# A routing stage takes over the experts' bias, the copy of x, the spare rows and the first weight load

## The chip, the cores and the metric

The program runs on one NeuronCore of a Trainium2 chip, as one launch. The metric is the device time of that core in microseconds (us), a median over executions. A profile is one execution as the hardware recorded it. The engines are TensorE (PE; its weight loads are PEld), VectorE (DVE), ScalarE (ACT), GpSimd (POOL) and SyncE (SP), which here only issues transfers. They run apart from each other and meet at semaphores.

## The reference

1250 tokens with 768 numbers each go through four residual blocks: a graph attention net, a mixture of experts, a graph convolution net and an attention block with a feed-forward net. The change lies in the second one:

```python
def _L0_ffn_ref(x, router_w, w1, b1, w2, b2):
    E, C, F, K = (8, 768, 384, 2)
    logits = flat @ router_w.T
    probs = jax.nn.softmax(logits.astype(jnp.float32), axis=-1)
    top_w, top_i = jax.lax.top_k(probs, K)
    top_w = (top_w / top_w.sum(-1, keepdims=True)).astype(x.dtype)
    out = jnp.zeros_like(flat)
    for e in range(E):
        w_e = jnp.sum(top_w * (top_i == e), axis=-1)[:, None]
        h = jax.nn.gelu(flat @ w1[e] + b1[e], approximate=False)
        out = out + w_e * (h @ w2[e] + b2[e])

x = x + _L0_ffn_ref(_layernorm(x, axis=-1)[None], L0_ffn_router_w, ...)[0]
```

Each token goes to two of eight experts. The term with `b2` needs no expert's product: for all tokens it is the matrix of weights (1250 x 8) times `b2` (8 x 768).

## The kernel before

The program is a row of stages. A stage (`Phase`) has its own tiles and semaphores, hands each engine a list of instructions, and ends at a barrier of all engines (`ph.end`): no engine starts the next stage before all have finished this one. Inside an engine's list the order is as written; there is no scheduler.

The tokens lie as 10 tiles of 125 rows (`NT`, `TP`). x, the residual, is kept in SBUF. `layernorm_turned` normalizes it, writes the rows to `token_scratch` in DRAM and keeps them turned for the router. Then come the two stages of the change.

`route` (lines 1147 to 1350) computes the logits on PE, the softmax and the two highest experts on DVE, and gives every choice a slot. The slots are cut into parts of 128 rows; two parts (`PER_LOAD`) share one load of an expert's weights, so that there are at most 17 loads and 34 parts. Which expert a load needs is in `load_expert` (L1319). PE turns the weights, and ACT copies them to `weights_T` (L1262) after POOL has cleared that tile (L1206). The last work of the stage is a loop of 20 steps, one for each tile of tokens and choice. In each, DVE builds a one-hot of the row in its part (`row_hot`, L1339) and three one-hots of the part, times the token, times the gate and plain (`part_hot`, L1340 to L1342), and PE adds their product to bank 6 (L1247). There are two buffers: step n of DVE waits until PE has done step n-2 (`placed`). Four small DVE operations (L1346 to L1349) turn the sum into `slot_token`, the list by which rows are gathered and scattered.

`experts` (from L1353) starts with work that isn't an expert's. POOL clears `b2` and `zeros`; SP loads `b2` and stores the zeros as spare rows of `token_scratch` and `sum_scratch`; SP reads `load_expert` and issues the first weights (`w1` L1403, `b1` L1406, `w2` L1409). PE makes 20 products of 384 columns of `weights_T` and `b2` (L1498) in two banks by turns; DVE adds each to x (L1607, semaphore `b2_added`); SP stores each finished tile of x to `sum_scratch` (L82, L83 in `move_rows`). POOL gathers the rows of the first parts (L1431) after the spare rows have landed. PE turns the rows of parts 0 and 1 (L1455), waits for the last of the 20 additions, and starts the first product of part 0 (L103, called by `up`). ACT and DVE split weights into a high and a low part first (L1519 and L1577 for `w1`; L1533 and L1587 for the rows). From there each part runs up, gelu, down, and POOL adds its rows to `sum_scratch` by an indirect DMA (L1444), one after another.

A PE product of two float32 operands is recorded as two LDWEIGHTS and two MATMUL; float32r operands give one of each, and a product of split operands (`product`, L103) has three of those.

Of the kernel before, what the change touches and what calls it, by code (L numbers as in the profile page):

```python
# [7 lines left out]
ALU = mybir.AluOpType  # L8
ACT = mybir.ActivationFunctionType
# [8 lines left out]
N = 1250  # L18
# [1128 lines left out]
def route(nc, g, i):  # L1147
# [4 lines left out]
    ps, ident, xT, weights, weights_T = g["ps"], g["ident"], g["xT"], g["weights"], g["weights_T"]  # L1152
    rw = ph.sb("router_w", [128, KD, EXPERTS])
    logit_T = ph.sb("logit_T", [EXPERTS, N])
    logits_out, cleared = ph.sem("logits_out"), ph.sem("cleared")
# [21 lines left out]
    gate = ph.sb("gate", [TP, 2, NT])  # L1177
# [9 lines left out]
    part_hot = ph.sb("part_hot", [TP, 2, 3, PARTS])  # L1187
    ended = ph.sb("ended", [TP, LOADS, EXPERTS])
# [9 lines left out]
    with ph.block() as block:  # L1198

        @block.sync  # L1200
        def _(sp):
            sp.dma_start(rw[:], i["router_w"]).then_inc(rw_in, 16)

        @block.gpsimd
        def _(pool):
            pool.memset(weights_T[:], 0.0).then_inc(cleared, 1)  # L1206
# [17 lines left out]
        def _(pe):  # L1224
# [19 lines left out]
            pe.matmul(ps[0:TP, 5, 0:NT * EXPERTS], all_ones[:], marks, start=True, stop=True).then_inc(counted, 1)  # L1244
            for n in range(2 * NT):
                pe.wait_ge(hot_ready, n + 1)
                last = pe.matmul(ps[0:PART, 6, 0:3 * PARTS], row_hot[:, n % 2, :], part_hot[:, n % 2].rearrange("p k s -> p (k s)"),  # L1247
                                 start=n == 0, stop=n == 2 * NT - 1)
                last.then_inc(placed, 1)

        @block.scalar
        def _(a):
# [6 lines left out]
            a.wait_ge(cleared, 1)  # L1259
            for b in range(3):  # L1260
                n = 4 if b < 2 else 2
                last = a.activation(weights_T[0:EXPERTS, b * 4 * TP:(b * 4 + n) * TP], ps[0:EXPERTS, 1 + b, 0:n * TP], ACT.Copy)  # L1262
            last.then_inc(turned_out, 1)

        @block.vector
        def _(v):
# [52 lines left out]
            step(v.tensor_copy(load_expert[:], one_load[0:1, :]))  # L1319
            step(v.tensor_tensor(place[:], ps[0:TP, 4, 0:NT * EXPERTS].rearrange("p (t e) -> p t e", e=EXPERTS), start[:, 0:NT, :], ALU.add))  # L1320
# [8 lines left out]
            step(v.tensor_reduce(gate[:], picked[:], AX.X, ALU.add))  # L1329
# [4 lines left out]
            for n in range(2 * NT):  # L1334
# [18 lines left out]
def experts(nc, g, i, x, token_scratch, sum_scratch, ahead):  # L1353
# [4 lines left out]
    ps, ident, weights_T = g["ps"], g["ident"], g["weights_T"]  # L1358
# [7 lines left out]
    b2 = ph.sb("b2", [128, D])  # L1366
    zeros = ph.sb("zeros", [128, D])
# [6 lines left out]
    cleared, b2_in, w1_in, w2_in, b1_in, ahead_in, x_stored, spare_stored = (  # L1374
        ph.sem("cleared"), ph.sem("b2_in"), ph.sem("w1_in"), ph.sem("w2_in"), [ph.sem("b1_in0"), ph.sem("b1_in1")],
        ph.sem("ahead_in"), ph.sem("x_stored"), ph.sem("spare_stored"))
    w1_high, w2_high, w1_split, w2_split = ph.sem("w1_high"), ph.sem("w2_high"), ph.sem("w1_split"), ph.sem("w2_split")
    b2_done, b2_added = ph.sem("b2_done"), ph.sem("b2_added")
# [11 lines left out]
    with ph.block() as block:  # L1390

        @block.sync
        def _(sp):
            sp.wait_ge(cleared, 2)
            sp.dma_start(b2[0:EXPERTS, :], i["moe_b2"]).then_inc(b2_in, 16)
            sp.dma_start(token_scratch[N:N + PART, :], zeros[:]).then_inc(spare_stored, 16)
            sp.dma_start(sum_scratch[N:N + PART, :], zeros[:]).then_inc(spare_stored, 16)

            def load(n):
# [3 lines left out]
                sp.dma_start(w1, i["moe_w1"][bass.ds(e, 1)].rearrange("a (k p) f -> p (a k) f", p=128)).then_inc(w1_in, 16)  # L1403
# [5 lines left out]
                sp.dma_start(w2, i["moe_w2"][bass.ds(e, 1)].rearrange("a (k p) f -> p (a k) f", p=128)).then_inc(w2_in, 16)  # L1409

            load(0)
            for t in range(NT):
                sp.wait_ge(b2_added, 2 * t + 2)
                move_rows(sp, sum_scratch[t * TP:(t + 1) * TP, :], x[:, t, :], x_stored)
            for n in range(1, LOADS):
                load(n)
# [6 lines left out]
        def _(pool):  # L1423
            pool.memset(b2[:], 0.0).then_inc(cleared, 1)
            pool.memset(zeros[:], 0.0).then_inc(cleared, 1)
            pool.wait_ge(spare_stored, 32)
# [9 lines left out]
            for n in range(PARTS):  # L1436
# [3 lines left out]
                if n == 0:  # L1440
                    pool.wait_ge(x_stored, 32 * NT)
# [7 lines left out]
        def _(pe):  # L1449
# [41 lines left out]
            pe.wait_ge(cleared, 1)  # L1491
            pe.wait_ge(b2_in, 16)
            for t in range(NT):
                for j in range(2):
                    n = 2 * t + j
                    if n >= 2:
                        pe.wait_ge(b2_added, n - 1)
# [75 lines left out]
        def _(v):  # L1573
# [29 lines left out]
            for t in range(NT):  # L1603
                for j in range(2):
# [1164 lines left out]
```

## Time and profile before

| | us |
|---|---|
| median of 3 runs | 3139.02 (3132.99 to 3140.41) |
| the profiled execution, its own time | 3143.17 |
| its span in the trace | 3141.4 |
| PE busy in the span | 2598.8 (83%) |
| DVE busy | 1970.2 (63%) |
| ACT busy | 1393.8 (44%) |
| route, from its first POOL operation to its last on DVE | 1405.0 to 1464.2 |
| experts, from its first POOL operation | from 1466.4 |

Times in the trace count from the start of the span. The page of the profile sums each engine over the whole program; the chain of waits at its end covers only the last few per cent, so the two stages have to be read from the timeline and from the busy times of short windows. A stage ends at a barrier, so an engine that finishes early in it gains nothing by itself.

### The profile page before, as it was taken

How to read it: one execution, taken by the hardware profiler on the slowest of the kernel's cores; microseconds unless marked ns; L12 is line 12 of the kernel's file. 1: busy time of each engine (PE TensorE's matmuls, PEld its weight loads, DVE VectorE, ACT ScalarE, POOL GpSimd, SP SyncE). 2: the span in 40 equal slices, each digit the busy share in tenths (PEclk: the TensorE clock that was granted, in tenths of full speed). 3: DMA queues.
4: the chain of work that ended last, by engine and by line, in shares of the span. 5: the costliest groups of instructions: out<-in, count | busy, mean ns of one | idle time of the engine just before them, and what ended most of it. 6: DMA issues, size and time to landing. Idle time of an engine off the chain costs nothing. (4 is left out here: it accounts for less than half of the span.)

```text
span 3141.4 us, 40088 instructions
## 1 busy us (share of the span) xinstructions
PE 2598.8 (83%) x14620; PEld 2306.3 (73%) x14621; DVE 1970.2 (63%) x2887; ACT 1393.8 (44%) x2433; POOL 262.5 (8%) x190
## 2 busy tenths in 40 slices
PE   5774879887986978975999589789897998999876
PEld 5663779787986977963889557467665776999766
DVE  7776278787877843346555342542895556989654
ACT  0353267676775831110666310031896103777330
POOL 0000030040040000000232120000000000111000
PEclk9996989998998988986999779889998997999988
DMA  0023101201111262222899750124661212443304
GB/s 33 16 49 93 42 23 40 64 31 62 41 43 51 63 166 50 49 60 106 249 256 249 176 109 0 49 96 154 140 129 27 94 54 57 106 88 87 93 1 103
DMA packets 107249, 267.12 MB, mean 85 GB/s; under 512 B 11062, under 2 KB 49448, under 8 KB 106090
## 3 DMA queue, kind: packets, MB, share of 16 engines
q1 hardware_dynamic: 99474, 238.26, 27.8%
q0 software_dynamic: 7616, 26.74, 3.9%
q8 instruction: 99, 1.62, 0.2%
q14 instruction: 60, 0.49, 0.1%
HBM read 194.41 MB, written 66.73 MB: 83 GB/s over the span
## 5 line engine op out<-in xcount | busy, mean ns | idle before, releaser
L910 PE MATMUL ps<-h,e_gat_aggregate 125*125 125x193 f32 x2400 | 405.0, 332 | 51.9 <-DVE e_gat_aggregate L892 51.9
L910 PEld LDWEIGHTS ps<-h,e_gat_aggregate 125*125 125x125 f32 x2400 | 398.7, 191 | 58.2 <-DVE e_gat_aggregate L892 58.2
L890 DVE TENSOR_TENSOR e_gat_aggregate<-e_gat_aggregate 125x1250 f32<-125x1250 f32 x120 | 174.7, 1456 | 77.5 <-ACT e_gat_aggregate L861 74.3
L103 PE MATMUL ps<-gat_w_pair_gat_scores,x_turned 128*125 128x384 f32 x1080 | 195.7, 344 | 32.0 <-DVE gat_w_pair_gat_scores L757 31.9
L103 PEld LDWEIGHTS ps<-gat_w_pair_gat_scores,x_turned 128*125 128x125 f32 x1080 | 194.2, 190 | 33.3 <-DVE gat_w_pair_gat_scores L757 33.1
L103 PE MATMUL ps<-w_pair_dense_rows_from,col_dense_rows_from 128*125 128x384 f32 x1080 | 210.5, 352 | 8.3 <-DVE w_pair_dense_rows_from L1088 4.5
L103 PEld LDWEIGHTS ps<-w_pair_dense_rows_from,col_dense_rows_from 128*125 128x125 f32 x1080 | 196.3, 194 | 9.8 <-DVE col_dense_rows_from L1082 7.7
L858 ACT ACTIVATE e_gat_aggregate<-row_gat_aggregate,from_src 125x1250 f32<-125x1250 f32 x120 | 161.7, 1347 | 87.2 <-PE ps L910 62.6
L2448 DVE TENSOR_TENSOR ln_home<-p_attend,p_high_attend 125x1254 fp32r<-125x1254 f32 x120 | 179.9, 1512 | 27.1 <-ACT p_high_attend L2434 24.3
L2426 ACT ACTIVATE p_attend<-ps 125x1254 f32<-125x1254 f32 (+2 forms) x168 | 148.6, 915 | 79.9 <-PE ps L2389 78.1
L1941 DVE TENSOR_SCALAR_CACHE_REDUCE res_attention_statistics<-ps 125x1250 f32<-125x1250 f32 x120 | 173.3, 1459 | 12.2 <-PE ps L1918 6.2
L892 DVE SCALAR_TENSOR_TENSOR e_gat_aggregate<-e_gat_aggregate,count 125x1250 f32<-125x1250 f32 x120 | 175.3, 1461 | 4.2
L103 PE MATMUL ps<-V_home,ln_home 128*125 128x512 f32 x720 | 170.0, 398 | 2.7 <-PEq L54 2.7
L1965 ACT ACTIVATE p_attention_statistics<-res_attention_statistics,eak_attention_statistics 125x1250 bf16<-125x1250 f32 x120 | 160.7, 1339 | 14.8 <-DVE res_attention_statistics L1941 4.3
L508 PE MATMUL ps<-ident,_normed_layernorm_turned 125*128 125x125 f32 x300 | 69.5, 410 | 115.4 <-DVE _normed_layernorm_turned L493 115.3
L766 DVE SCALAR_TENSOR_TENSOR peak_gat_scores<-ps,from_src,peak_gat_scores 125x1250 f32<-125x1250 f32 x108 | 156.6, 1512 | 12.4 <-ACTq L730 12.3
L103 PEld LDWEIGHTS ps<-V_home,ln_home 128*125 128x125 f32 x720 | 135.1, 188 | 36.9 <-issue 2.8
L861 ACT ACTIVATE e_gat_aggregate<-row_gat_aggregate,from_src 125x1250 f32<-125x1250 f32 x120 | 160.1, 1334 | 1.3 <-DMA row_gat_aggregate<-r_scratch 1.3
L103 PE MATMUL ps<-ln_home,V_home 128*128 128x512 f32 (+3 forms) x702 | 142.5, 367 | 14.7 <-DVE V_home L613 14.7
L508 PEld LDWEIGHTS ps<-ident,_normed_layernorm_turned 125*128 125x128 f32 x300 | 55.8, 217 | 129.0 <-DVE _normed_layernorm_turned L493 129.0
L103 PEld LDWEIGHTS ps<-ln_home,V_home 128*128 128x128 f32 (+1 forms) x702 | 118.4, 195 | 38.9 <-DVE V_home L613 15.2
L351 PE MATMUL ps<-dst_hot_build_adjacency,src_hot_build_adjacency 125*125 125x128 bf16 x1600 | 122.8, 230 | 25.9 <-DVE dst_hot_build_adjacency L283 25.9
(388 smaller groups left out, 5119.3 us busy)
## 6 DMA issues: line engine op xcount, KB each, us to landing
stock<-in_moe_w SPq DMA_DIRECT2D x34, 1152.0 KB, 6.9
row_gat_aggregate<-r_scratch SPq DMA_DIRECT2D x24, 625.0 KB, 6.1
V_home<-q_scratch SPq DMA_DIRECT2D x44, 312.5 KB, 6.3
ln_home<-q_scratch SPq DMA_DIRECT2D x36, 312.5 KB
ln_home<-k_scratch SPq DMA_DIRECT2D x36, 312.5 KB
rows_dense_rows_from<-node_scratch SPq DMA_DIRECT2D x8, 1080.0 KB
q_scratch<-V_home SPq DMA_DIRECT2D x6, 1250.0 KB, 4.6
k_scratch<-V_home SPq DMA_DIRECT2D x6, 1250.0 KB, 4.6
```

The lines of the kernel that those rows point to most:

```text
L103: last = pe.matmul(out, left(x), right(y), start=start and n == 0, stop=stop and n == 2)
L508: last = pe.transpose(ps[:, 2 * (t % 4) + k // 4, k % 4 * TP:(k % 4 + 1) * TP], normed[:, t % 3, k * 128:(k + 1) * 128], ident[0:TP, 0:TP])
L766: last = v.scalar_tensor_tensor(peak[:, head, :], far[t % 2], from_src[:, head, t:t + 1], peak[:, head, :], ALU.subtract, ALU.min)
L858: a.activation(e[:, n % 3, 0, :], row[0:TP, head % 2, 0, :], ACT.Exp, bias=from_src[:, head, t:t + 1])
L861: a.activation(e[:, n % 3, 1, :], row[0:TP, head % 2, 1, :], ACT.Exp, bias=from_src02[:, head, t:t + 1]).then_inc(exp_ready, 1)
L890: v.tensor_tensor(e[:, n % 3, 0, :], e[:, n % 3, 0, :], e[:, n % 3, 1, :], ALU.max).then_inc(p_step, 1)
L892: v.scalar_tensor_tensor(e[:, n % 3, 0, :], e[:, n % 3, 0, :], 1.0, count[:, t, 0:N], ALU.min, ALU.mult).then_inc(p_ready, 1)
L910: last = pe.matmul(ps[0:TP, bank(head, d // 2), d % 2 * (C + 1):(d % 2 + 1) * (C + 1)], e[:, n % 3, 0, d * TP:(d + 1) * TP], h[:, t, head, :],
L1941: v.tensor_scalar(minus[:, n % 3, :], flat(n), 1.0, None, ALU.mult, ALU.min, accum_out=peak[:, head, t:t + 1]).then_inc(peaked, 1)
L1965: a.activation(p[:], minus[:, n % 3, :], ACT.Exp, scale=-1.0, bias=peak[:, head, t:t + 1], accum_out=total[:, head, t:t + 1]).then_inc(sum ...
L2426: last = a.activation(spread(p[:, n % AHEAD, :])[:, at:end, :], ps[0:TP, bank:bank + end - at, 0:PIECE], ACT.Exp, scale=-1.0)
L2448: v.tensor_tensor(p_low[:, n % AHEAD, :], p[:, n % AHEAD, :], p_high[:, n % AHEAD, :].bitcast(F32), ALU.subtract).then_inc(split, 1)
```

## The change

The 20 products of weights and `b2` go to `route`. They are no longer added to x by DVE: PE adds x itself, by a product of the identity with x into the same bank (L1272 of the new kernel), and ACT copies the sum back to x (L1300). Eight of the 20 stand before the loop of 20 steps, twelve inside it, each ahead of a step's product. They rotate over four banks. SP loads `b2` (now 8 rows) at the stage's start, stores the spare rows, waits for `load_expert` and issues the first `w1` and `w2`, and then stores x tile by tile; it waits for all stores at the stage's end. In the step of the loop the three one-hots of the part become one `scalar_tensor_tensor` with the factors token, gate and 1, which a MEMSET, a copy and the former reduction of the gates put side by side. `experts` loses its whole preamble and starts with the gathers; only `b1` of the first load is still issued there.

```diff
+            sp.dma_start(b2[:], i["moe_b2"]).then_inc(b2_in, 16)
+            sp.wait_ge(zeroed, 1)
+            sp.dma_start(token_scratch[N:N + PART, :], zeros[:]).then_inc(stored, 16)
+            sp.dma_start(sum_scratch[N:N + PART, :], zeros[:]).then_inc(stored, 16)
+            sp.wait_ge(load_known, 1)
+            e = sp.value_load(load_expert[0:1, 0:1], min_val=0, max_val=EXPERTS - 1)
+            sp.dma_start(stock(g, 0, KD, FF), i["moe_w1"][bass.ds(e, 1)]...).then_inc(g["w1_in"], 16)
+            sp.dma_start(stock(g, KD * FF, FF // 128, D), i["moe_w2"][bass.ds(e, 1)]...).then_inc(g["w2_in"], 16)
+            for t in range(NT):
+                sp.wait_ge(x_out, 2 * t + 2)
+                move_rows(sp, sum_scratch[t * TP:(t + 1) * TP, :], x[:, t, :], stored)
+            sp.wait_ge(stored, 32 + 32 * NT)
...
-            pool.memset(weights_T[:], 0.0).then_inc(cleared, 1)
+            pool.memset(zeros[:], 0.0).then_inc(zeroed, 1)
...
+            def with_bias(n):
+                t, j = n // 2, n % 2
+                if n >= 4:
+                    pe.wait_ge(x_out, n - 3)
+                columns = slice(j * 384, (j + 1) * 384)
+                out = ps[0:TP, X_BANKS[n % 4], 0:384]
+                pe.matmul(out, weights_T[:, t * TP:(t + 1) * TP], b2[:, columns], start=True, stop=False)
+                pe.matmul(out, ident[0:TP, 0:TP], x[:, t, columns], start=False, stop=True).then_inc(x_summed, 1)
+
+            pe.wait_ge(b2_in, 16)
+            pe.wait_ge(turned_out, 1)
+            for n in range(8):
+                with_bias(n)
             for n in range(2 * NT):
+                if n + 8 < 2 * NT:
+                    with_bias(n + 8)
                 pe.wait_ge(hot_ready, n + 1)
...
+            for n in range(2 * NT):
+                a.wait_ge(x_summed, n + 1)
+                a.activation(x[:, n // 2, n % 2 * 384:(n % 2 + 1) * 384], ps[0:TP, X_BANKS[n % 4], 0:384], ACT.Copy).then_inc(x_out, 1)
...
-                v.tensor_scalar(part_hot[:, n % 2, 0], part_iota[:], here, token[:, t:t + 1], ALU.is_equal, ALU.mult)
-                v.tensor_scalar(part_hot[:, n % 2, 1], part_iota[:], here, gate[:, c, t:t + 1], ALU.is_equal, ALU.mult)
-                step(v.tensor_scalar(part_hot[:, n % 2, 2], part_iota[:], here, None, ALU.is_equal))
+                step(v.scalar_tensor_tensor(part_hot[:, n % 2], part_iota[:].unsqueeze(1).broadcast_to([TP, 3, PARTS]), here,
+                                            factor[:, c, t, :].unsqueeze(2).broadcast_to([TP, 3, PARTS]), ALU.is_equal, ALU.mult))
...
-            pe.wait_ge(cleared, 1)
-            pe.wait_ge(b2_in, 16)
-            for t in range(NT):
-                for j in range(2):
...
-                    pe.matmul(ps[0:TP, 6 + j, 0:384], weights_T[:, t * TP:(t + 1) * TP], b2[:, j * 384:(j + 1) * 384],
-                              start=True, stop=True).then_inc(b2_done, 1)
             turn(0)
             turn(1)
-            pe.wait_ge(b2_added, 2 * NT)
...
-            for t in range(NT):
-                for j in range(2):
-                    v.wait_ge(b2_done, 2 * t + j + 1)
-                    here = x[:, t, j * 384:(j + 1) * 384]
-                    v.tensor_tensor(here, ps[0:TP, 6 + j, 0:384], here, ALU.add).then_inc(b2_added, 1)
```

PE's list from the counting of the choices to the first product of an expert, before (x20 stands for the 20 steps, which nothing separates):

```order
238 L1243 MATMUL ps<-either_route,tokens_before_route 125x80
239 L1244 MATMUL ps<-either_route,all_ones_route 125x80
240 L1247 MATMUL ps<-part_hot_route,row_hot_route 128x102 x20
241 L1198 UNCONDITIONAL_BRANCH
242 L1448 UNCONDITIONAL_BRANCH
243 L1498 MATMUL ps<-b_experts,expert_weights_T 125x384 x20
244 L1455 MATMUL ps<-ident,rows_experts 128x128 x12
245 L103 MATMUL ps<-w_pair_experts,rows_turned_experts 128x384 x18
```

And after, where the eight pairs ahead of the loop end and its steps begin:

```order
254 L1271 MATMUL ps<-b_route,weights_turned_route 125x384
255 L1272 MATMUL ps<-x,ident 125x384
256 L1271 MATMUL ps<-b_route,weights_turned_route 125x384
257 L1272 MATMUL ps<-x,ident 125x384
258 L1282 MATMUL ps<-part_hot_route,row_hot_route 128x102
259 L1271 MATMUL ps<-b_route,weights_turned_route 125x384
260 L1272 MATMUL ps<-x,ident 125x384
261 L1282 MATMUL ps<-part_hot_route,row_hot_route 128x102
```

```order
288 L1282 MATMUL ps<-part_hot_route,row_hot_route 128x102
289 L1271 MATMUL ps<-b_route,weights_turned_route 125x384
290 L1272 MATMUL ps<-x,ident 125x384
291 L1282 MATMUL ps<-part_hot_route,row_hot_route 128x102 x9
292 L1204 UNCONDITIONAL_BRANCH
293 L1470 UNCONDITIONAL_BRANCH
294 L1477 MATMUL ps<-ident,rows_experts 128x128 x12
295 L103 MATMUL ps<-w_pair_experts,rows_turned_experts 128x384 x18
```

Steps 0 to 11 now have a pair of 384-column products ahead of their own; the last eight have none; and the turning of rows follows the stage's start directly.

DVE's list at the first step of the loop, before:

```order
605 L1339 TENSOR_SCALAR row_hot_route<-row_iota_route,row_of_route 125x128
606 L1340 TENSOR_SCALAR part_hot_route<-part_iota_route,part_of_route,token_route 125x34
607 L1341 TENSOR_SCALAR part_hot_route<-part_iota_route,part_of_route,gate_route 125x34
608 L1342 TENSOR_SCALAR part_hot_route<-part_iota_route,part_of_route 125x34
609 L1339 TENSOR_SCALAR row_hot_route<-row_iota_route,row_of_route 125x128
```

and after:

```order
607 L1379 TENSOR_SCALAR row_hot_route<-row_iota_route,row_of_route 125x128
608 L1380 SCALAR_TENSOR_TENSOR part_hot_route<-part_iota_route,part_of_route,factor_route 125x102
609 L1379 TENSOR_SCALAR row_hot_route<-row_iota_route,row_of_route 125x128
```

A step has two operations in place of four; the new one covers 102 columns where each of the three old ones covered 34.

## Rows read from the trace of the kernel before

**Rows 1.** Busy time in windows; the column after POOL's is the granted clock.
```profile
1444.20:1463.20 19.00, 14.14 (x38) 9.51 (x38) 15.32 (x72) 0.00 (x0) 0.00 (x0) 0.50 0.00 0
...
1474.40:1486.70 12.30, 12.27 (x33) 4.83 (x33) 8.76 (x16) 2.59 (x6) 1.91 (x2) 1.00 0.98 380
...
1506.00:1545.00 39.00, 35.96 (x222) 35.09 (x221) 23.10 (x40) 25.61 (x51) 12.92 (x10) 1.00 0.91 254
```

**Rows 2.** Timeline (start, length, engine, line), before the loop of steps.
```profile
1433.53 1.30 ACT L1262 ACTIVATE expert_weights_T<-ps 8x500 f32<-8x500 f32 x3 [10.22 <-PE ps L1238]
...
1433.63 0.62 PE L1244 MATMUL ps<-either_route,all_ones_route 125*125 125x80 f32 x2
```

**Rows 3.** Timeline, one step of the loop on DVE and PE.
```profile
1453.64 0.29 DVE L1339 TENSOR_SCALAR row_hot_route<-row_iota_route,row_of_route 125x128 f32<-125x128 f32 x1 [0.15 <-DVE part_hot_route L1342]
...
1454.26 0.24 DVE L1342 TENSOR_SCALAR part_hot_route<-part_iota_route,part_of_route 125x34 f32<-125x34 f32 x1
1454.61 0.50 PEld L1247 LDWEIGHTS ps<-part_hot_route,row_hot_route 125*128 125x128 f32 x2 [0.50 <-DVEq L1343]
...
1454.65 0.29 DVE L1339 TENSOR_SCALAR row_hot_route<-row_iota_route,row_of_route 125x128 f32<-125x128 f32 x1 [0.15 <-DVE part_hot_route L1342]
```

**Rows 4.** Timeline, the end of route and the start of experts.
```profile
1462.62 0.75 PE L1247 MATMUL ps<-part_hot_route,row_hot_route 125*128 125x102 f32 x2 [0.25 <-DVEq L1343]
...
1464.03 0.17 DVE L1349 CAST slot_token<-filled_route 128x34 int32<-128x34 f32 x1
1466.44 0.74 POOL L1424 MEMSET b_experts<- 128x768 f32 x1 [58.33 <-POOLq L54]
...
1476.56 2.59 ACT L1519 ACTIVATE w_pair_experts<-stock 128x384 fp32r<-128x384 f32 x6 [41.73 <-DMA stock<-in_moe_w]
```

**Rows 5.** Timeline, DVE's first two additions of the bias, and PE's first ten matmuls.
```profile
1469.73 5.61 PE L1498 MATMUL ps<-b_experts,expert_weights_T 128*125 128x384 f32 x10 [6.36 <-DMA b_experts<-in_moe_b]
...
1471.38 0.56 DVE L1607 TENSOR_TENSOR x<-ps,x 125x384 f32<-125x384 f32 x1 [7.18 <-PE ps L1498]
...
1472.66 0.56 DVE L1607 TENSOR_TENSOR x<-ps,x 125x384 f32<-125x384 f32 x1 [0.72 <-PE ps L1498]
```

**Rows 6.** Timeline, from the turned rows to the first product of part 0.
```profile
1486.75 0.82 PE L1455 MATMUL ps<-ident,rows_experts 128*128 128x128 f32 x6
...
1487.42 2.89 DVE L1577 TENSOR_TENSOR w_pair_experts<-stock,w_pair_experts 128x384 fp32r<-128x384 f32 x6
...
1487.60 0.87 ACT L1533 ACTIVATE rows_turned_experts<-ps 128x512 fp32r<-128x512 f32 x2 [8.45 <-PE ps L1455]
...
1490.23 1.02 DVE L1587 TENSOR_TENSOR rows_turned_experts<-ps,rows_turned_experts 128x512 fp32r<-128x512 f32 x2
...
1491.39 1.51 PE L1455 MATMUL ps<-ident,rows_experts 128*128 128x128 f32 x6 [3.83 <-DVE rows_turned_experts L1587]
...
1492.56 5.60 PE L103 MATMUL ps<-w_pair_experts,rows_turned_experts 128*128 128x384 f32 x18
```

**Rows 7.** Groups of instructions by shape, whole span: count, busy us, mean ns of one.
```profile
L1743 PE MATMUL ps<-gcn_w,urned_graph_convolutions 128*125 128x384 f32 x80 | 26.9, 491 | 1.8 <-ACT urned_graph_convolutions L1757 1.3 <-DVE x L1797 0.4
...
L283 DVE SCALAR_TENSOR_TENSOR dst_hot_build_adjacency<-ion_iota_build_adjacency,_columns_build_adjacency,e_values_build_adjacency 125x128 bf16 x160 | 54.9, 343 | 0.0
...
L741 ACT ACTIVATE h<-ps 125x384 f32<-125x384 f32 x60 | 29.0, 484 | 29.2 <-PE ps L103 29.2
```

**Rows 8.** Granted clock in short windows, columns as in rows 1.
```profile
1473.25:1473.50 0.25, 0.25 (x2) 0.23 (x1) 0.00 (x0) 0.00 (x0) 0.20 (x1) 0.50 0.82 301
1473.50:1473.75 0.25, 0.25 (x2) 0.19 (x2) 0.00 (x0) 0.00 (x0) 0.25 (x1) 0.94 1.04 393
...
1497.00:1498.00 1.00, 1.00 (x6) 0.84 (x4) 0.47 (x1) 0.31 (x1) 0.00 (x0) 0.79 0.45 167
```

**Rows 9.** The 34 gathers of rows (L1431), us from issue to landing.
```profile
DMA to landing us min/median/max: 4.9/5.7/8.8
```

**Rows 10.** Issue of a plain transfer: KB, us to landing.
```profile
token_scratch<-zeros_experts SPq DMA_DIRECT2D x1, 384.0 KB, 2.3
```

More of the change, by code:

```diff
@@ L1144, with route @@
 PARTS = LOADS * PER_LOAD
-def route(nc, g, i):
+def route(nc, g, i, x, token_scratch, sum_scratch):
     ph = Phase(nc, g, "route")
-    ps, ident, xT, weights, weights_T = g["ps"], g["ident"], g["xT"], g["weights"], g["weights_T"]
+    ps, ident, xT, weights = g["ps"], g["ident"], g["xT"], g["weights"]
+    weights_T = ph.sb("weights_turned", [EXPERTS, N])
+    b2 = ph.sb("b2", [EXPERTS, D])
+    zeros = ph.sb("zeros", [128, D])
+    b2_in, zeroed, load_known, x_summed, x_out, stored = (
+        ph.sem("b2_in"), ph.sem("zeroed"), ph.sem("load_known"), ph.sem("x_summed"), ph.sem("x_out"), ph.sem("stored"))
+    X_BANKS = (7, 1, 2, 3)
     rw = ph.sb("router_w", [128, KD, EXPERTS])
     logit_T = ph.sb("logit_T", [EXPERTS, N])
-    logits_out, cleared = ph.sem("logits_out"), ph.sem("cleared")
+    logits_out = ph.sem("logits_out")
     lower = ph.sb("lower_index", [TP, EXPERTS, EXPERTS])
@@ L1258, in _ @@
             a.wait_ge(turned, 1)
[L1259 removed]
             for b in range(3):
                 n = 4 if b < 2 else 2
[L1262 removed]
+                last = a.activation(weights_T[:, b * 4 * TP:(b * 4 + n) * TP], ps[0:EXPERTS, 1 + b, 0:n * TP], ACT.Copy)
             last.then_inc(turned_out, 1)
+            for n in range(2 * NT):
+                a.wait_ge(x_summed, n + 1)
+                a.activation(x[:, n // 2, n % 2 * 384:(n % 2 + 1) * 384], ps[0:TP, X_BANKS[n % 4], 0:384], ACT.Copy).then_inc(x_out, 1)
         @block.vector
@@ L1328, in _ @@
             step(last)
-            step(v.tensor_reduce(gate[:], picked[:], AX.X, ALU.add))
+            v.memset(factor[:, :, :, 2], 1.0)
+            v.tensor_copy(factor[:, :, :, 0], token[:].unsqueeze(1).broadcast_to([TP, 2, NT]))
+            step(v.tensor_reduce(factor[:, :, :, 1], picked[:], AX.X, ALU.add))
             step(v.tensor_copy(slot_i[:, 0], slot[:]))
@@ L1350, in route, with experts @@
     ph.end()
-def experts(nc, g, i, x, token_scratch, sum_scratch, ahead):
+def experts(nc, g, i, token_scratch, sum_scratch, ahead):
     ph = Phase(nc, g, "experts")
-    ps, ident, weights_T = g["ps"], g["ident"], g["weights_T"]
+    ps, ident = g["ps"], g["ident"]
     slot_token, slot_gate, load_expert = g["slot_token"], g["slot_gate"], g["load_expert"]
@@ L1408, in load @@
                     sp.wait_ge(w2_split, KF * n)
-                sp.dma_start(w2, i["moe_w2"][bass.ds(e, 1)].rearrange("a (k p) f -> p (a k) f", p=128)).then_inc(w2_in, 16)
-            load(0)
-            for t in range(NT):
-                sp.wait_ge(b2_added, 2 * t + 2)
-                move_rows(sp, sum_scratch[t * TP:(t + 1) * TP, :], x[:, t, :], x_stored)
-            for n in range(1, LOADS):
+                    sp.dma_start(w2, i["moe_w2"][bass.ds(e, 1)].rearrange("a (k p) f -> p (a k) f", p=128)).then_inc(w2_in, 16)
+            for n in range(LOADS):
                 load(n)
@@ L2647, in build @@
             g["weights"] = tile(moe, "expert_weights", [TP, NT, EXPERTS])
-            g["weights_T"] = tile(moe, "expert_weights_T", [128, N])
+            g["w1_in"] = moe.enter_context(nc.semaphore("first_layer_in"))
+            g["w2_in"] = moe.enter_context(nc.semaphore("second_layer_in"))
             g["slot_token"] = tile(moe, "slot_token", [PART, PARTS], I32)
@@ L2654, in build @@
                 layernorm_turned(nc, g, x, g["xT"], stats_there=True, rows_to=token_scratch)
-                route(nc, g, i)
-            experts(nc, g, i, x, token_scratch, sum_scratch, ahead=[(i["q_w"], 0)])
+                route(nc, g, i, x, token_scratch, sum_scratch)
+            experts(nc, g, i, token_scratch, sum_scratch, ahead=[(i["q_w"], 0)])
         with ExitStack() as gcn:
```

30 lines of the change are left out of this document (9 added, 21 removed).

## The prediction

> **What bounds the kernel now.** I read the timeline first, since the change touches two neighbouring stages and nothing else, and a stage ends at a barrier: what counts is when route's last engine finishes, and how long experts then takes to its first product. The reader should see three things. First, route's end is the loop of 20 steps, and DVE paces it: a step starts every 1.01 us (1453.64 to 1454.65, [rows 3]), PE is busy for 14.1 of 19 us there at a granted clock of 0.50, which is the level of 1.2 GHz [rows 1], and ACT and the DMA do nothing. Second, the first product of an expert starts at 1492.56 [rows 6], 26.1 us after experts' first operation at 1466.44 [rows 4]. That time is the preamble: PE and DVE pass the bias back and forth until 1486.7, then come turned rows and their split. Third, once the parts run, PE is busy for 36.0 of 39 us [rows 1], so whatever the head gains or loses is carried to the end, give or take how the transfers happen to meet.
>
> So there are two terms: A, how much later route ends, and B, how much shorter experts' head is.
>
> **Term A: route with 20 pairs of products in it.** The pairs can start when ACT has copied the turned weights, at 1433.53 + 1.30 = 1434.83 [rows 2]; with a semaphore's 0.1 us, at 1434.95. A pair is two float32 products, four recorded matmuls of 384 columns. At half clock, a product that was two such matmuls followed the last one by 1472.66 - 1471.38 = 1.28 us [rows 5], 0.64 us for each; at full clock that is 0.32, and a dense group of the same width ran 26.9 / 80 = 0.336 us for each [rows 7]. I take 0.33: 80 x 0.33 = 26.3 us. Between the pairs stand steps 0 to 11, each a product of 102 columns whose two weight loads took 0.50 us at half clock [rows 3]; at full clock I take 0.25: 3.0 us.
>
> PE starts this at half clock, as the whole stretch was. The clock rose 3.8 us after the bias products began (1469.73 to 1473.5, [rows 5, 8]) and 6.4 us after turned rows and the first expert's product began (1491.39, to about 1497.4 within the last window, [rows 6, 8]). Here PE is dense too, so it should rise after 3.8 to 6.4 us; half of that time is lost, 1.9 to 3.2, I take 2.5. Step 11 is then done at 1434.95 + 26.3 + 3.0 + 2.5 = 1466.75. Step 0's one-hots are ready long before PE comes to them, and the DVE edit hides behind PE for the first twelve steps; the two added small DVE operations do too.
>
> The last eight steps are paced by DVE again. Its step was three operations started 0.207 us apart (0.62 over three, [rows 3]), the last one's 0.24, and 0.15 to the next. The new step is one such start, the merged operation and 0.15. The nearest row for the merged one is a scalar_tensor_tensor of 128 columns, 0.343 us [rows 7]; 26 columns less make about 0.32. A step: 0.207 + 0.32 + 0.15 = 0.68 us. Step 12 is prepared by then; steps 13 to 19 take 7 x 0.68 = 4.8 us, with 0.1 ahead and 0.7 for the last product: the last matmul ends at 1472.3. Before it ended at 1462.62 + 0.75 = 1463.37 [rows 4]. **A = +8.9 us.**
>
> Its ends: with 0.32 for a matmul, 0.2 for a step's product, 1.9 lost to the clock and steps of 0.63, it ends at 1469.5, +6.1. With 0.35, 0.4, 3.2 and steps of 0.86 (PE falling back to half clock, where its product comes into the two-buffer cycle), at 1477.9, +14.5.
>
> What lies beside this: ACT's copy of a pair is about 0.48 us [rows 7] against 1.3 for the pair, with four banks, so it holds up nobody. SP waits for x's last store before the barrier; that store is issued about 0.6 us after the last pair, at about 1467.2, and 384 KB landed in 2.3 us [rows 10], so it is in by 1470 and would become the stage's end only beyond about 5.5 us of landing. The first weights are issued as soon as `load_expert` is known, before the loop of steps, and have all of it to land. Ahead of the router's product SP issues the small router_w before anything else, so I cost the 768 KB of spare rows at nothing (at most 0.5 us if they hold it up). POOL's memset is smaller than the one it replaces.
>
> **Term B: experts' head.** Of the 26.1 us, the new head keeps: the gather, the turning, ACT's high part, DVE's low part, the second turning. SP, POOL, PE and DVE lose all that stood ahead. The weights' split (2.59 us on ACT from the stage's start, DVE 2.89 a little behind, [rows 4, 6]) is over before rows arrive. POOL issues at once, 0.2 us in. How long a gather takes on an idle DMA the trace doesn't show: under load it was 4.9 us at least, 5.7 in the middle, 8.8 at most [rows 9]; a plain store of the same 384 KB took 2.3 [rows 10]. I take the least of the loaded ones, 4.9, since only b1 moves beside it. Then, with PE at half clock after its pause: turned rows 1.51 instead of 0.82, then ACT 0.87, DVE 1.02, and 1.17 + 0.14 from there to the first product by way of the second turning (1491.25 to 1492.56, [rows 6]), with small gaps 4.8 us. Sum: 0.2 + 4.9 + 4.8 = 9.9 us. **B = 9.9 - 26.1 = -16.2 us**, and -18.8 with a gather of 2.3, -12.3 with 8.8. The first expert's product ran at half clock before (5.60 us, [rows 6]) and will again.
>
> The page "DMA: Bandwidth & Descriptors" of the Trainium skill (Anatomy of one DMA) fits a transfer issued by GpSimd as 2.0 us plus the bytes at 436 GB/s; for these 384 KB that is an estimate of 2.9 us. The trace's own least is 4.9 on a loaded DMA, so no row here shows the lower figure; by the page the sum below would be 2.0 us lower.
>
> **The sum.** -16.2 + 8.9 = -7.3 us, against the profiled 3143.17: 3135.9. That execution lies 4.2 us above the median of 3139.02, and the change should move both alike: 3131.7, **3132**. The program after the head is the same list; one gather that meets other traffic differently can shift it by up to 8.8 - 4.9 = 3.9 us either way [rows 9].
>
> **The rivals.** (1) The cheap ends hold: PE's loop at +6.1, a gather that lands in 2.3 us, -18.8. That gives -12.7, 3126. For it: the DMA is idle when experts starts. Against it: no gather here took less than 4.9 us. (2) The work is only moved: PE's stretch costs +14.5 and the gather 8.8 us, -12.3; together +2.2, 3141. For it: the identity product doubles the matmuls (80 for 40) where DVE had added for nothing while PE was the slower partner. Against it: only both ends together cancel. (3) Slower: PE stays at half clock in route. Every window of its loop stood at 0.50 [rows 1], and the eight pairs might not change that. Then 80 x 0.64 + 12 x 0.5 + 7 x 0.86 + 0.8 = 64 us put the end at 1499.0, A = +35.6, and the total at +19.4, 3158. It decides by time at half clock: each us of it costs 0.5, so beyond the 5 us that I allow another 15 bring the sum to zero, and 33 bring it 0.3% above. Against it: under the same products at the start of experts the clock did rise, and stood at 1.00 for 12 us [rows 1, 8], with PE less dense than here. (4) The merge doesn't do what it says: a broadcast operand makes 102 columns cost as much as the three old ones. Then the last seven steps take 1.0 us each, +2.3, 3134: inside the range.
>
> **How the numbers follow.** About 0.3% (9.4 us) is what a measurement of this kernel can tell from no change. My forecast, a sum between -9.4 and -3, has 0.50. Rival 1, a gain above 9.4, has 0.32. Rival 2 and its neighbourhood, -3 to +9.4, has 0.14. Rival 3 has 0.04. Rival 4 is part of the first. So faster 0.32, same 0.64, slower 0.04. The range reaches from rival 1 with one lucky gather (3124) to rival 2 (3141): it leaves out rival 3 and thin ends on both sides, less than 2 in 10.
>
> **What would show it.** In the changed profile: pairs of bias and x products starting at about 1434.9, the granted clock at 1.00 from about 1440 to 1466, a pair and a step every 1.55 us; steps 12 to 19 every 0.7 us; route's last product ending near 1472.3; experts' first operation near 1475.5; first product of an expert about 10 us behind it, at half clock; and from there the parts at their old pace. It would be wrong if the clock stays at 0.50 in the pairs, if x's last store lands after the slot list is done, if the first gather takes under 3 or over 7 us, or if the loop over parts has other waits for its gathers than before.

## The result, and the profile after

| | before | after |
|---|---|---|
| median, us | 3139.72 (3132.99 to 3145.14, 4 runs) | 3168.25 (3167.41 to 3174.61, 4 runs) |
| the profiled execution's span | 3141.4 | 3165.7 |
| last matmul of route ends | 1463.37 | 1508.1 |
| experts' first operation | 1466.44 | 1511.55 |
| first product of an expert starts | 1492.56 | 1521.96 |
| next stage after experts starts | 1787.59 | 1812.18 |

The change made the kernel slower: the ratio is 1.0098, with a 95% interval of 1.0085 to 1.0112, or 28.5 us. The forecast was 3132, with a range up to 3141. Slower had 0.04.

Read the table downwards. Route ends 44.7 us later. From route's last matmul to the first product took 29.2 us and now takes 13.9, so the first product comes 29.4 us later. The next stage comes 24.6 us later and the span ends 24.3 us later. So the head of experts got shorter nearly as forecast, and the whole loss is route's. The first view to open is the granted clock. These are windows of the kernel after; the columns are busy time (and count) of PE, weight loads, DVE, ACT and POOL, then the granted clock, the DMA share and GB/s.

```profile
1435.00:1440.00 5.00, 5.00 (x7) 1.76 (x8) 4.13 (x23) 0.49 (x1) 0.00 (x0) 0.50 0.00 0
1440.00:1460.00 20.00, 20.00 (x26) 6.00 (x25) 3.18 (x16) 2.95 (x6) 0.00 (x0) 0.50 0.52 176
1460.00:1480.00 20.00, 20.00 (x34) 9.23 (x34) 2.60 (x10) 2.95 (x6) 0.00 (x0) 0.50 0.22 58
1480.00:1500.00 20.00, 20.00 (x36) 9.44 (x34) 3.13 (x12) 2.95 (x6) 0.00 (x0) 0.50 0.22 58
1500.00:1508.00 8.00, 7.75 (x21) 5.11 (x20) 3.65 (x14) 0.49 (x1) 0.00 (x0) 0.50 0.18 48
```

PE is busy without a pause from 1435 to 1500, and its clock stands at 0.50, the level of 1.2 GHz, in every window. Under the bias products of the kernel before, at the head of experts, it had risen after 3.8 us [rows 5, 8] and stood at 1.00 [rows 1]. The timeline of PE at the start of the new products shows a second loss. L1271 is the bias product, L1272 the product that adds x by the identity:

```profile
1434.93 1.61 PE L1271 MATMUL ps<-b_route,weights_turned_route 8*125 8x384 f32 x2 [0.72 <-ACT weights_turned_route L1296]
1436.47 1.64 PE L1272 MATMUL ps<-x,ident 125*125 125x384 f32 x2
1438.04 1.64 PE L1271 MATMUL ps<-b_route,weights_turned_route 8*125 8x384 f32 x2
1439.61 1.64 PE L1272 MATMUL ps<-x,ident 125*125 125x384 f32 x2
```

A product starts every 1.57 us. Before, at the same half clock, it was every 1.28 us [rows 5]. The 0.29 us more are weight loads that no matmul covers. In the loop of steps the timeline, here with the weight loads (PEld), shows it at each change of operand:

```profile
1482.75 0.49 PEld L1272 LDWEIGHTS ps<-x,ident 125*125 125x125 f32 x2 [1.08 <-issue]
1482.75 1.64 PE L1272 MATMUL ps<-x,ident 125*125 125x384 f32 x2
...
1484.70 0.49 PEld L1271 LDWEIGHTS ps<-b_route,weights_turned_route 8*125 8x125 f32 x2 [0.18 <-issue]
1484.71 1.64 PE L1271 MATMUL ps<-b_route,weights_turned_route 8*125 8x384 f32 x2
1484.81 0.29 DVE L1379 TENSOR_SCALAR row_hot_route<-row_iota_route,row_of_route 125x128 f32<-125x128 f32 x1 [3.01 <-PE ps L1282]
...
1488.23 0.49 PEld L1271 LDWEIGHTS ps<-b_route,weights_turned_route 8*125 8x125 f32 x2 [0.18 <-issue]
```

The load of a product and its first matmul start together; a load that lay under the matmul ahead would start earlier. The first load of L1271 is in the same place at 1484.70 and 1488.23: a pair and a step take 3.53 us, where 1.55 was forecast. DVE, which paced this loop before [rows 3], now waits 3.01 us in each step for PE. Last, the end of route and the head of experts in the timeline of after:

```profile
1507.36 0.50 PEld L1282 LDWEIGHTS ps<-part_hot_route,row_hot_route 125*128 125x128 f32 x2 [0.25 <-DVEq L1382]
...
1508.78 0.17 DVE L1388 CAST slot_token<-filled_route 128x34 int32<-128x34 f32 x1
1511.55 2.59 ACT L1531 ACTIVATE w_pair_experts<-stock 128x384 fp32r<-128x384 f32 x6 [9.00 <-PEq L54]
...
1512.32 1.38 POOL L1455 DMA_INDIRECT rows_experts<-token_scratch,slot_token  x1 [104.69 <-POOLq L54]
...
1517.14 1.54 PE L1477 MATMUL ps<-ident,rows_experts 128*128 128x128 f32 x6 [9.02 <-DMA rows_experts<-token_scratch,slot_token]
...
1521.96 1.31 PE L103 MATMUL ps<-w_pair_experts,rows_turned_experts 128*128 128x384 f32 x3
```

The last step's load starts at 1507.36 and its matmuls take 0.75 as in [rows 4], hence 1508.1. The first gather is issued at 1512.32, and its rows are turned from 1517.14. The first product follows 10.4 us behind ACT's first operation, against 26.1 in the kernel before [rows 4, 6].

### The profile page after: what moved, and what is told of

The parts are those of the page before. It is cut to its first block and busy times, and to the rows that moved or that the text cites. A ratio compares the mean times of both kernels' runs of the same rounds, so it can differ in the third digit from the quotient of the medians.

```text
span 3165.7 us, 40130 instructions
## 1 busy us (share of the span) xinstructions
PE 2636.1 (83%) x14660; PEld 2316.2 (73%) x14661; DVE 1952.8 (62%) x2829; ACT 1404.8 (44%) x2453; POOL 264.2 (8%) x188
```

## The experiments

Two theories were open. **Rows**: a bias product has an operand of 8 rows ("8*125"), where the one before had 128; products of few rows don't lift the clock, and they leave the loads uncovered. **Place**: route's mixture of work (ACT's copies, the steps, the DMA of x and of the first weights) holds the clock down, whatever the operands. The expectations call Rows theory 1; they split Place into the identity product (rival 2) and the uncovered loads or the steps between the pairs (rival 3).

**e1_pad: the kernel after with the bias product's operands padded to 128 rows.**

```diff
-    weights_T = ph.sb("weights_turned", [EXPERTS, N])
-    b2 = ph.sb("b2", [EXPERTS, D])
+    weights_T = ph.sb("weights_turned", [128, N])
+    b2 = ph.sb("b2", [128, D])
...
+            pool.memset(b2[:], 0.0).then_inc(cleared, 1)
+            pool.memset(weights_T[:], 0.0).then_inc(cleared, 1)
```

> The changed kernel with one thing undone: the turned weights and the bias are again 128-row tiles with 120 rows of zeros (two more memsets on POOL), so that the first product of each pair uses 128 rows and not 8. Theory 1 (the 8-row operand kept the granted clock at 0.50): the clock rises to 1.00 about 4 to 6 us after the first pair, a pair and a step take 1.6 us, the last product of route ends near 1472 instead of 1508, and the time is near 3132 us. Rival 2 (the identity product keeps it there) and rival 3 (the exposed weight loads or the steps between the pairs keep it there): the clock stays at 0.50 and the time at 3168 us.

Measured: 3132.76 us against 3137.8, ratio 0.9983 (0.9972 to 0.9994). Its windows:

```profile
1435.00:1440.00 5.00, 4.29 (x7) 2.39 (x8) 4.18 (x23) 1.05 (x3) 0.00 (x0) 0.52 0.00 2
1440.00:1455.00 15.00, 15.00 (x53) 9.08 (x52) 5.80 (x26) 5.39 (x11) 0.00 (x0) 1.00 0.81 286
1455.00:1470.00 15.00, 13.74 (x59) 8.84 (x57) 6.41 (x25) 3.93 (x8) 0.00 (x0) 1.00 0.49 129
```

and its timeline, PE's start and the end of route:

```profile
1437.12 1.48 PE L1276 MATMUL ps<-x,ident 125*125 125x384 f32 x2
1438.40 1.48 PE L1275 MATMUL ps<-b_route,weights_turned_route 128*125 128x384 f32 x2
1439.68 0.87 PE L1276 MATMUL ps<-x,ident 125*125 125x384 f32 x2
...
1471.15 0.50 PEld L1286 LDWEIGHTS ps<-part_hot_route,row_hot_route 125*128 125x128 f32 x2 [0.18 <-DVEq L1387]
```

The same instructions with 120 more rows of zeros run at the full clock from about 1440. Even before it rises the products are 1.28 us apart (1437.12 to 1438.40), so the loads are covered again. The last step's matmuls end at 1471.15 + 0.75 = 1471.9, the first product starts at 1485.97. Place had forecast no change and fell. What counts here is how many rows the instruction addresses: 120 rows of zeros did for the clock what it had lost. Since padding also covers the loads, this run doesn't tell whether the rows themselves or the uncovered loads held the clock down; e2_before_8rows does.

**e2_before_8rows: the kernel before, its bias product alone with 8 rows.** If rows alone do it, it must show in the old place too.

```diff
-                    pe.matmul(ps[0:TP, 6 + j, 0:384], weights_T[:, t * TP:(t + 1) * TP], b2[:, j * 384:(j + 1) * 384],
+                    pe.matmul(ps[0:TP, 6 + j, 0:384], weights_T[0:EXPERTS, t * TP:(t + 1) * TP], b2[0:EXPERTS, j * 384:(j + 1) * 384],
```

> The kernel before, where only the 20 bias products at the start of experts take 8 rows of the same two tiles and not 128. Theory 1: the clock, which rose 3.8 us after their start, stays at 0.50 through them; they take 20 x 1.28 us or more and not 17, so experts' first product starts 8 to 14 us later, 3148 to 3153 us. Rivals 2 and 3: nothing changes, 3139 us, since there is no identity product and no step between.

Measured: 3146.9 us, ratio 1.0034 (1.0024 to 1.0044), 9.1 us more; in the trace the first product of an expert starts 9.2 us later, at 1501.73. A window of it:

```profile
1475.00:1485.00 10.00, 10.00 (x16) 4.84 (x16) 4.30 (x8) 2.59 (x6) 1.91 (x2) 0.50 1.01 391
```

and the group of L1498 (busy us, mean ns of one, idle before):

```profile
L1498 PE MATMUL ps<-b_experts,expert_weights_T 8*125 8x384 f32 x40 | 25.9, 845 | 6.3 <-DMA b_experts<-in_moe_b 6.3
```

The same forty matmuls took 17.1 us at 561 ns with 128 rows. Here all operands have 8 rows, nothing alternates, and the loads are covered (the twenty products fill 25.9 us, about 1.29 each, without a gap). So the clock stays down with no uncovered load: they are two effects.

**e6_64rows and e7_32rows: padded to 64 and to 32 rows only** (`weights_T[0:64, ...], b2[0:64, ...]` and `0:32` in the product of e1_pad).

> The padded kernel, but the bias product takes 64 of the 128 rows. One look at the granted clock. If it is only the few live rows of an operand that keep the clock down, it should still rise with 64 rows beside the 125 of the identity product, later than with 128; the kernel before gives a hint against it, its product of 64 rows at line 2215 ran at 844 ns for a matmul, the half clock's length. Rises: 3133. Stays: 3165.

> The same with 32 rows. Theory 1 expects the clock to stay at 0.50 as with 8, 3165 us; if 32 rows beside the identity's 125 suffice, it rises, 3133 us, and a quarter of the padding would have done.

Measured: 3167.9 and 3169.51 us, like the kernel after. The window 1475 to 1500 of e6_64rows:

```profile
1475.00:1500.00 25.00, 25.00 (x43) 11.87 (x44) 3.96 (x16) 3.49 (x8) 0.00 (x0) 0.50 0.23 62
```

and its bias matmuls (least, median and longest in ns):

```profile
L1275 PE MATMUL ps<-b_route,weights_turned_route x40: 841/908/1001, 1435.6 to 1500.3; 64*125 64x384 f32 x40
```

The medians of a matmul are 908 and 906 ns, as the 906 with 8 rows. Half of the rows didn't help in anything. Each is one execution, but both lie over 30 us above the slowest of e1_pad's ten. These two runs have e1_pad's memsets and its later load of `b2` as well, so those aren't what brought the clock back there.

**e3_identity_alone: the bias products left out** (the result then lacks the bias); only the identity product of 125 rows stays, `start=True`.

> The changed kernel without the bias product of each pair (the bias is left out of the result), so that only the identity product stands in its place. Theory 1: every product left has 125 or 128 rows and the clock rises within about 6 us. Rival 2: it stays at 0.50 through the 20 identity products. At half clock they take 20 x 0.7 x 2 = 28 us with the steps, at full clock about 16.

Measured: 3130.72 us. Its windows:

```profile
1438.00:1442.00 4.00, 3.28 (x8) 1.86 (x8) 2.86 (x17) 1.55 (x4) 0.00 (x0) 0.50 0.00 0
1442.00:1445.00 3.00, 3.00 (x9) 1.64 (x8) 2.54 (x12) 1.60 (x4) 0.00 (x0) 0.74 0.00 0
1445.00:1455.00 10.00, 10.00 (x44) 6.46 (x43) 6.98 (x30) 6.15 (x13) 0.00 (x0) 1.00 0.91 318
```

The products start at 1439.2 and the clock rises within 1442 to 1445 (0.50 until 1443, 1.00 from 1444): with half of the matmuls, in the same place and beside the same traffic, it isn't held down. The identity product isn't the cause.

**e8_two_by_two and e9_four_by_four: the kernel after with 8 rows, the products in another order**: two bias products, then their two identity products; or four and four.

```diff
+                for m in range(n, n + 4):
+                    pe.matmul(ps[0:TP, X_BANKS[m % 4], 0:384], weights_T[:, ...], b2[:, ...], start=True, stop=False)
+                for m in range(n, n + 4):
+                    pe.matmul(ps[0:TP, X_BANKS[m % 4], 0:384], ident[0:TP, 0:TP], x[:, ...], start=False, stop=True)
```

> The changed kernel with 8 rows, the same products in another order: two bias products, then their two identity products, for every second step. In the changed kernel each product starts 1.57 us after the last where 4 x 320 ns at full clock or 1.28 at half would be the columns' time. If the 0.29 us come from changing between an operand of 8 rows and one of 125, half of the 40 changes go and route's pairs take about 5.8 us less at the same half clock: 3162 us. If each weight load is exposed whatever stands ahead, nothing changes: 3168 us.

> The changed kernel with 8 rows, in groups of four: four bias products, then their four identity products. With two by two the clock rose after all, 35 us in. If what lifts it is a stretch of full-row products as dense as the 3.8 us of the preamble before, the identity stretches (4 x 1.28 = 5.1 us at half clock) should lift it in the first or second of them, 1440 to 1452, and the bias stretches may drop it again: 3140 to 3150 us. If only the average share counts, it rises as late as with two by two or never: 3148 to 3160 us. The exposed 0.29 us should now appear 10 times and not 40.

e8_two_by_two took 3152.9 us. PE's timeline:

```profile
1436.19 2.89 PE L1272 MATMUL ps<-b_route,weights_turned_route 8*125 8x384 f32 x4 [0.72 <-ACT weights_turned_route L1300]
1439.01 2.92 PE L1275 MATMUL ps<-x,ident 125*125 125x384 f32 x4
```

and two windows:

```profile
1470.00:1475.00 5.00, 5.00 (x18) 2.91 (x17) 1.08 (x5) 1.71 (x4) 0.00 (x0) 0.87 0.29 77
1475.00:1485.00 10.00, 10.00 (x37) 5.63 (x36) 3.09 (x12) 2.78 (x7) 0.00 (x0) 1.00 0.44 117
```

Two products take 2.82 to 2.86 us: 2.56 and 0.29 once instead of twice. So an uncovered load belongs to each change between the two row counts. (The expectation sets 4 x 320 ns for a product at full clock; a product is two matmuls, and in e1_pad it took 0.65 us.) The clock did rise here, which the expectation didn't foresee and which makes the time 9 us less than its 3162, but only some 35 us after the first product. Once up, it stayed at 1.00 from 1475 to 1485, although half of the 384-column products there have 8 rows. e9_four_by_four, 3149.95 us, shows the clock following the rows within one stream. First its windows:

```profile
1443.00:1448.00 5.00, 5.00 (x9) 2.47 (x8) 3.23 (x16) 1.38 (x3) 0.00 (x0) 0.50 0.66 205
1448.00:1449.00 1.00, 1.00 (x3) 0.23 (x2) 0.00 (x0) 0.21 (x2) 0.00 (x0) 0.55 1.07 416
1449.00:1452.00 3.00, 3.00 (x9) 1.49 (x9) 0.00 (x0) 0.37 (x1) 0.00 (x0) 1.00 1.02 386
1452.00:1453.00 1.00, 1.00 (x4) 0.53 (x3) 0.00 (x0) 0.41 (x1) 0.00 (x0) 0.65 0.96 384
1453.00:1455.00 2.00, 2.00 (x5) 1.08 (x4) 0.00 (x0) 0.57 (x2) 0.00 (x0) 0.50 0.19 77
```

and PE's timeline:

```profile
1437.98 5.45 PE L1271 MATMUL ps<-b_route,weights_turned_route 8*125 8x384 f32 x8 [0.72 <-ACT weights_turned_route L1299]
1443.36 5.48 PE L1274 MATMUL ps<-x,ident 125*125 125x384 f32 x8
1448.77 2.88 PE L1271 MATMUL ps<-b_route,weights_turned_route 8*125 8x384 f32 x8
1451.59 4.54 PE L1274 MATMUL ps<-x,ident 125*125 125x384 f32 x8
```

PE never pauses in these windows. After 5.4 us of 125-row products the clock rises; the next bias products run at full clock (2.8 us), and it falls at about 1452.3, 0.7 us into the next products of 125 rows. It follows what PE did shortly before, and a block of 8-row products acts on it as PE's idle 5 us do in e5_pool_adds below. Of all runs this is the plainest, though it is one execution.

**e4_merge_alone: the kernel before with the merged one-hots only**, to price the second part of the change by itself.

```diff
-                v.tensor_scalar(part_hot[:, n % 2, 0], part_iota[:], here, token[:, t:t + 1], ALU.is_equal, ALU.mult)
-                v.tensor_scalar(part_hot[:, n % 2, 1], part_iota[:], here, gate[:, c, t:t + 1], ALU.is_equal, ALU.mult)
-                step(v.tensor_scalar(part_hot[:, n % 2, 2], part_iota[:], here, None, ALU.is_equal))
+                step(v.scalar_tensor_tensor(part_hot[:, n % 2], part_iota[:]. ... , here, factor[:, c, t, :]. ... , ALU.is_equal, ALU.mult))
```

> The kernel before with only the merged one-hots (factor tile and one operation for three). A step then takes 0.68 us and not 1.01, or 0.7 to 0.8 where PE at half clock comes into the cycle: 20 x 0.25 to 0.33 = 5 to 6.6 us less, 3133 to 3134 us. If the merge did nothing: 3139.

The weight loads of its steps in the timeline:

```profile
1449.95 0.50 PEld L1247 LDWEIGHTS ps<-part_hot_route,row_hot_route 125*128 125x128 f32 x2 [0.25 <-DVEq L1344]
1450.62 0.50 PEld L1247 LDWEIGHTS ps<-part_hot_route,row_hot_route 125*128 125x128 f32 x2 [0.17 <-DVEq L1344]
1451.38 0.50 PEld L1247 LDWEIGHTS ps<-part_hot_route,row_hot_route 125*128 125x128 f32 x2 [0.25 <-DVEq L1344]
```

Measured: 3134.84 us, ratio 0.9986 (0.9977 to 0.9996). Steps come every 0.67 and 0.76 us by turns instead of every 1.01 [rows 3]. From the first step's matmuls to the end of the last (1447.10 to 1461.4) the loop takes 14.3 us, and 20.1 in the kernel before (1443.24 to 1463.37): 5.9 us less, as expected. The medians differ by 3.0 only. **e11_pad_no_merge** is the reverse, e1_pad with the three operations put back:

> The padded kernel with the three separate one-hots again. PE paces the first twelve steps, so only the last seven cost more, 7 x 0.33 = 2.3 us: the last product ends near 1474.2 and the time is near 3135 us. If the merge matters in the first twelve too, up to 6 us more.

One execution took 3130.9 us, which says nothing beside e1_pad's 3125 to 3136. In the trace its last load starts at 1472.83 and e1_pad's at 1471.15; its route began 0.3 us earlier, so the merge is worth about 2 us with the products in place. Its last eight steps are again 1.00 us apart.

**e5_pool_adds: can PE be spared the identity products?** e1_pad without them: ACT copies the bias to SBUF, POOL adds it to x.

```diff
+                pool.wait_ge(copied, n + 1)
+                pool.tensor_tensor(here, bias_rows[:, n % 4, :], here, ALU.add).then_inc(x_out, 1)
```

> The padded kernel of the first run (128-row operands), and x is no longer added by PE's identity product: ACT copies each bias product to SBUF and POOL, idle there, adds it to x; SP's stores wait for POOL. PE's 80 matmuls of 384 columns become 40, 13 us less at full clock. If PE's stretch is what ends route, step 11 ends near 1454 and DVE paces the rest, so the last product ends near 1460 instead of 1471.9 and the time is 12 us below the padded kernel, 3120 us. Rival: POOL's additions (no row of their cost; if over 1.5 us each) end the stage, 3125 to 3132. Rival: PE is not dense enough between DVE's steps and falls back to half clock, 3125.

Measured: 3132.89 us against 3139.84, ratio 0.9981 (0.9971 to 0.9991): no better than e1_pad beyond the noise (0.9983), so the 12 us that were expected didn't come. A window:

```profile
1445.00:1450.00 5.00, 0.18 (x1) 0.00 (x0) 4.64 (x13) 0.55 (x2) 3.68 (x4) 0.78 0.57 163
```

and two groups:

```profile
L1250 POOL TENSOR_TENSOR x<-bias_rows_route,x 125x384 f32<-125x384 f32 x20 | 19.6, 1001 | 35.7 <-ACT bias_rows_route L1312 35.6
...
L1359 DVE TENSOR_TENSOR lower_span_route<-lower_index_route,span_route 125x64 f32<-125x64 f32 x1 | 1.0, 992 | 0.0
```

with, from the timeline, one of DVE's additions that takes an input from PSUM:

```profile
1445.05 0.24 DVE L1370 TENSOR_TENSOR place_route<-ps,start_route 125x80 f32<-125x80 f32 x1
```

Beside POOL's addition of 1.00 us, DVE's small addition with both inputs in SBUF takes 992 ns; in e1_pad it took 225. The one with an input in PSUM stood beside POOL's additions too and kept its 0.24 us. DVE reached its first one-hot 13.0 us after PE's first bias product, against 7.5 in e1_pad, so PE stood idle from 1445 to 1450 and lost its clock again (0.53 in the 5 us behind). The page "SBUF — State Buffer" of the Trainium skill (SBUF: two separate sides) says that DVE and GpSimd share a pair of ports as an exclusive lock, held for a whole instruction, also when a DVE operation has two inputs in SBUF. The trace agrees for these two additions. Some operations with one input were stretched as well: the CAST that writes `load_expert` took 914 ns, and 167 in e1_pad.

**e10_shared: a better version.** Padded as e1_pad; four pairs ahead of the loop instead of eight, one in each of steps 0 to 15, and from the sixth on DVE adds x to every second one from PSUM (0.56 us, one input in PSUM), so that PE has eight identity products fewer.

```diff
+    by_vector = list(range(5, 2 * NT, 2))
...
+                    v.tensor_tensor(here, ps[0:TP, X_BANKS[m % 4], 0:384], here, ALU.add).then_inc(x_added, 1)
```

> The padded kernel, with PE's stretch shortened without POOL: four pairs ahead of the loop and one in each of steps 0 to 15; for every second of those in the loop DVE adds x from PSUM (0.56 us after its step) and PE's identity product is left out. PE: 1437.5 + 13.1 + 5 + 12 x 0.655 = 1463.5 for step 15, four steps of DVE alone behind it, last product near 1466 instead of 1471.9. 6 us below the padded kernel, 3127 us. Rival: DVE, now 0.68 + 0.6 us in every second step, or PE dropping to half clock between, gives it back: 3132 us.

Its windows:

```profile
1440.00:1455.00 15.00, 15.00 (x55) 9.23 (x55) 10.52 (x45) 3.93 (x8) 0.00 (x0) 0.93 0.68 243
1455.00:1468.00 13.00, 11.45 (x49) 7.36 (x47) 8.47 (x29) 1.97 (x4) 0.00 (x0) 1.00 0.66 198
```

Measured: 3129.39 us against 3141.47 of the kernel before, ratio 0.9960 (0.9946 to 0.9974), some 2 us above what was expected. It is faster than both the kernel before and the one after. Its last matmul ends at about 1468.0, though in that execution its route began some 3 us later than before's; from the first bias product to there it takes 29.7 us, and e1_pad 36.2, so the stretch is shorter by the 6 us that were expected. Each against the kernel before that was measured beside it, e10_shared gains 12.1 us and e1_pad 5.0, some 7 apart.

## Why the prediction was wrong

**The step that failed** is the clock in term A: "Here PE is dense too, so it should rise after 3.8 to 6.4 us". It didn't rise in 66 us. The two rises that this was read from had products of 128 rows [rows 5, 6]; the new ones have 8 rows, and the prediction never weighed that. e1_pad, e2_before_8rows, e3_identity_alone and e9_four_by_four show it from four sides: padding alone brings the clock back, few rows alone take it away in the old place, the 125-row products alone lift it (within about 4 us), and in one stream it goes up and down with them.

**The second miss** is the size of a matmul. Rival 3 had the clock right and put the end at +35.6; measured is +44.7. It took 0.64 us for each of 80 matmuls. The products came every 1.57, not 1.28, us: 40 x 0.29 = 11.6 more. Its steps of 0.5 were 3.53 - 3.14 = 0.39 (12 x 0.11 = 1.3 less), its last steps of 0.86 about 0.7 (1.1 less). Together 9.2, the difference. No row of before that the prediction used had two row counts by turns. The effect is shown by e8_two_by_two, which halves it, and by e1_pad and e2_before_8rows, which don't have it.

**The evidence was there.** The trace of before holds dense products of 24 rows, which the prediction didn't read. First a window of it:

```profile
1840.00:1850.00 10.00, 10.00 (x15) 4.65 (x14) 4.16 (x3) 0.00 (x0) 0.00 (x0) 0.50 0.62 122
```

and the line's matmuls (least, median and longest in ns, first and last start, forms):

```profile
L1643 PE MATMUL ps<-low_adapter,adapter_wu x36: 502/1056/1056, 1836.9 to 1859.8; 24*128 24x512 f32 x24, 24*128 24x226 f32 x12
```

PE is busy for 10.00 of 10 us at 0.50, having come in at full clock (0.84 in the window 1836 to 1840), and it is so again from 1850 to 1860. The fall itself follows 1.4 us in which PE was idle, so what this line shows is that 20 us of dense 24-row products don't lift the clock. "Against it: under the same products at the start of experts the clock did rise" called products the same that differ in rows.

**What held.** With the rows padded, term A is what the prediction said: last matmul at 1471.9 (1472.3 forecast), clock at 1.00 from 1440, a pair and a step in 1.51 us (1.55). That it is so near is in part luck: the pairs began at 1435.71, 0.8 us later than forecast, and the steps' products, 0.20 us and not 0.25, gave 0.6 back. Term B: 10.4 us (9.9 forecast), in it a gather of 4.8 us from issue to the first turned row (4.9 forecast); the 0.5 more are POOL's issue, 0.77 us behind ACT's first operation where 0.2 was taken. The estimate of 2.9 us from the page "DMA: Bandwidth & Descriptors" of the Trainium skill (Anatomy of one DMA) isn't borne out by the trace, which has 4.8. The merged operation took 320 ns (0.32), so rival 4 falls. x's last stores were issued at 1502.9, well ahead of the slot list's end. e1_pad's first product comes 6.6 us earlier than before's, where the sum said 7.3, and the medians differ by 5.0. One sum of the prediction is off: the cheap end of term A adds up, from its own terms, to 1470.1 and +6.7, not 1469.5 and +6.1, which makes rival 1 3127 us and not 3126. Nothing else rests on it.

**What stays open.** From the first product of an expert to the next stage the kernel before took 295.0 us and the one after 290.2, which gives back 4.8 of the 29.4 us. In the other traces this stretch took between 287.3 us (e1_pad) and 296.5 (e3_identity_alone) with the new head, 290.7 at most without that one, 289.0 (e2_before_8rows) and 293.7 (e4_merge_alone) with the old one. The two ranges overlap, so it isn't the head by itself. POOL's waits for the scatter of results don't follow it either: 55.7 us in 9 waits before (295.0 us), 43.5 in 7 after (290.2), 57.0 in 10 in e1_pad (287.3). The prediction had allowed 3.9 us either way for one gather that meets other traffic; which transfer it is was not tried. Open too is why the clock rose in e8_two_by_two after some 35 us and never in the kernel after: e8_two_by_two has the same products with half of the uncovered loads. And open is why it then stayed up, with 8-row blocks of 1.5 us, while in e9_four_by_four it fell after blocks of 2.8.

## What to carry to other kernels

Price a matmul moved or rewritten at the clock that its own operands earn, by the row count of both: a small contraction that is filled with zeros up to 128 rows costs two memsets and no time on PE, and was worth about 35 us here against 8 rows. In a trace of before, look for a dense stretch of the same row count and read its granted clock before forecasting one. And an addition that goes from DVE to PE or POOL isn't free because the engine looks idle: on PE it cost two more matmuls for each product, 0.64 us apiece at half clock, and on POOL it stretched DVE's operations beside it from about 0.2 to 1 us.

## What the hardware showed that I hadn't expected

- PE busy for 20.00 of 20 us stayed at the granted clock 0.50 for 66 us when every second product had 8, 32 or 64 rows; with 128 rows, 120 of them zero, it rose about 4 us after the first product (e1_pad). The page "TensorE: Matmul & The Clock Gate" of the Trainium skill (What's actually happening) says that activity releases the throttle, by how busy PE has been, and doesn't speak of rows. Taken as busy time in a profile, the rule would have given 1.00 here; the trace doesn't agree.
- At half clock, products of 8, 32 or 64 rows by turns with products of 125 start every 1.57 us; 128 by turns with 125, or 8 alone, every 1.28. So 0.29 us of load is uncovered at each change (the kernel after, e6_64rows, e7_32rows; e1_pad and e2_before_8rows).
- A POOL addition of 125x384 float32 in SBUF takes 1.00 us and stretches a DVE addition of 125x64 beside it, with both inputs in SBUF, from 0.23 to 0.99 us; one with an input in PSUM kept 0.24.
